# A state-space scan in 64 states: three of four time blocks summed in PSUM instead of two, and one PSUM bank for the other products in the loop

## The reference

```python
xz = rmsnorm(x, rms_w) @ in_proj            # xi | z, 512 channels each
xi = silu(causal_conv4(xi))                 # depthwise, 4 taps
dt, Bm, Cm = split(xi @ x_proj)             # 16 | 16 | 16
delta = softplus(dt @ dt_w + dt_b)
h[t] = exp(delta[t] * A) * h[t-1] + (delta[t] * xi[t]) * Bm[t]    # per channel, per state s = 0..15
y[t] = sum over s of h[t, s] * Cm[t, s]
y = (y + xi * D) * silu(z)
x = x + y @ out_proj                        # then attention and FFN
```

## Time and profile before

| | us |
|---|---|
| three runs | 591.8, 594.72, 595.92 |
| median | 594.72 |
| the profiled execution | 597.62 |
| its span, first to last instruction | 595.8 |
| mean granted TensorE clock of it | 0.899 |

### The profile page before, as it was taken

The page is one execution under the profiler, slowest core; times in us unless marked ns, Lnnn a source line. Parts: engine busy times, 40 slices in busy tenths (PEclk is TensorE's granted clock), DMA queues, the critical chain, the costliest instruction groups (busy, mean ns, idle before and its releaser), DMA issues. The chain is left out here.

```text
span 595.8 us, 7810 instructions
## 1 busy us (share of the span) xinstructions
PE 489.1 (82%) x2733; PEld 346.1 (58%) x2733; DVE 488.7 (82%) x576; ACT 354.8 (60%) x618; POOL 352.9 (59%) x212
## 2 busy tenths in 40 slices
PE   5877898779778999896689998956977777999882
PEld 5522765455566667554566765646866466787631
DVE  4858999997999899989988898899999899732413
ACT  4566667668765767886667678876466476400300
POOL 5007979756885698777938987776577645000000
PEclk9997999976889999779999996899998888796985
DMA  8221101111101011010110111012012910073004
GB/s 289 93 71 56 53 36 36 38 37 35 36 35 36 34 39 39 35 36 36 37 36 35 36 38 37 35 36 71 31 40 86 402 54 1 1 286 129 1 0 147
DMA packets 17919, 38.87 MB, mean 65 GB/s; under 512 B 1666, under 2 KB 10498, under 8 KB 17875
## 3 DMA queue, kind: packets, MB, share of 16 engines
q1 hardware_dynamic: 17874, 38.32, 18.4%
HBM read 36.08 MB, written 2.23 MB: 64 GB/s over the span
## 5 line engine op out<-in xcount | busy, mean ns | idle before, releaser
L1259 POOL TENSOR_TENSOR scanmem<-par,scanmem 128x1024 f32<-128x1024 f32 x128 | 299.3, 2363 | 111.9 <-PE hT L759 64.2
L1130 ACT ACTIVATE dA<-par,Aneg 128x512 f32<-128x512 f32 x256 | 172.5, 690 | 70.7 <-DVE scanmem L1583 69.7
L759 PE MATMUL hT<-con,scanmem 128*128 128x128 f32 x1024 | 160.5, 295 | 57.1 <-DVE yTd L1599 34.7
L759 PEld LDWEIGHTS hT<-con,scanmem 128*128 128x128 f32 x1024 | 123.3, 150 | 116.5 <-DVE yTd L1599 47.4
L1583 DVE TENSOR_TENSOR_SCAN scanmem<-dA,carry,scanmem 128x512 f32<-128x512 f32 x128 | 156.9, 1268 | 2.5 <-ACT dA L1130 2.4
L1583 DVE TENSOR_TENSOR_SCAN scanmem<-dA,scanmem 128x512 f32<-128x512 f32 x128 | 149.3, 1209 | 3.4 <-ACT dA L1130 3.0
L1140 ACT ACTIVATE hc<-hT,CTs 128x512 f32<-128x512 f32 x128 | 87.3, 682 | 77.0 <-PE hT L759 76.3
L1599 DVE SCALAR_TENSOR_TENSOR yTd<-hT,CTs,yTd 128x512 f32<-128x512 f32 x120 | 87.9, 732 | 9.8 <-PE hT L759 9.6
L543 PE MATMUL yacc<-con,hc 128*128 128x128 f32 x512 | 79.1, 298 | 5.8 <-ACT hc L1140 5.8
L487 PE MATMUL pp<-xnT,wi 128*128 128x512 f32 x128 | 66.8, 655 | 7.7 <-ACT xnT L927 4.0
L543 PEld LDWEIGHTS yacc<-con,hc 128*128 128x128 f32 x512 | 65.2, 154 | 9.9 <-ACT hc L1140 6.5
(11 more groups left out here) (169 smaller groups left out, 467.7 us busy)
## 6 DMA issues: line engine op xcount, KB each, us to landing
scanmem<-brow SPq DMA_DIRECT2D x32, 512.0 KB, 3.6
par<-in SPq DMA_DIRECT2D x1, 4096.0 KB, 16.7
scanmem<-in SPq DMA_DIRECT2D x1, 4096.0 KB, 14.5
xt<-in SPq DMA_DIRECT2D x4, 512.0 KB, 6.7
wi<-in SPq DMA_DIRECT2D x2, 1024.0 KB, 7.8
out<-par SPq DMA_DIRECT2D x4, 512.0 KB, 3.9
aw<-in SPq DMA_DIRECT2D x5, 256.0 KB, 6.5
xr<-in SPq DMA_DIRECT2D x1, 1024.0 KB, 9.5
```

Of the source, the lines that this page charges most:

```text
L759: last = nc.tensor.transpose(hT[:, i % 2, m * P:(m + 1) * P], hb[:, n % RING, m, i * P:(i + 1) * P], ident)
L1130: A(dA[:, m % 2, :], delta(c)[:, m, :], ACT.Exp, scale=Aneg[:, m * NS + s:m * NS + s + 1]).then_inc(da_ready, 1)
L1259: nc.gpsimd.tensor_tensor(hb[:, n % RING, ms, :], dx(c)[:, ms, :], Bb[:, row:row + 1, :].to_broadcast([P, 2, T]), ALU.mult).then_inc(bx_re ...
```

## The change

Blocks 0, 1 and 2 are now scaled by ScalarE (three mul_steps a state) and summed by TensorE in three yacc banks (BY_ACT = 3); block 3 alone is summed by VectorE, behind scan 3. mul_step reads hT[i % 2], and the third scaled tile lies in yTd. The Y job of block 1 is gone; the gate products of state 0 are three. The third yacc bank is taken from pp: pp is one bank, and in the loop each job waits for the read of the job before it (held_before). Ahead of the loop the jobs alternate with yacc[2], behind it with dA[1]. The tables move the jobs to other slots.

```diff
-PROLOGUE = {3: [("T", 0), ("T", 1)], 4: [("I", 0)], 5: [("I", 1)], 6: [("I", 2)], 7: [("I", 3)], 8: [("V", 0)],
-            10: [("V", 2)], 12: [("V", 3)], 14: [("X", 0)], 18: [("XT", 0), ("D", 0)], 20: [("D", 1), ("D", 2)], 21: [("D", 3)],
-            22: [("Z", 0)], 23: [("Z", 1)], 24: [("Z", 2)], 25: [("Z", 3)]}
-EPILOGUE = {1: [("Y", 1), ("Y", 3)], 11: [("O", 0)], 16: [("O", 1)], 28: [("R", 0)], 30: [("R", 1)]}
+PROLOGUE = {4: [("T", 0)], 5: [("T", 1)], 6: [("I", 0)], 7: [("I", 1)], 8: [("I", 2)], 9: [("I", 3)], 11: [("V", 0)],
+            13: [("V", 2)], 15: [("V", 3)], 17: [("X", 0)], 18: [("XT", 0)], 19: [("D", 0)], 20: [("D", 1)], 21: [("D", 2)],
+            22: [("D", 3)], 25: [("Z", 0)], 26: [("Z", 1)], 27: [("Z", 2)], 28: [("Z", 3)]}
+EPILOGUE = {1: [("Y", 3)], 2: [("O", 0)], 23: [("O", 1)], 29: [("R", 0)], 31: [("R", 1)]}
...
+def held_before(q):
+
+    if q < LOOP_FIRST or q > TAIL_FIRST + 1:
+        return [ORDER[q - 2]] if q >= 2 else []
+    if q == LOOP_FIRST:
+        return [ORDER[q - 2], ORDER[q - 1]]
+    return [ORDER[q - 1]] if q <= TAIL_FIRST else []
...
-        yacc = ctx.enter_context(nc.psum_tensor("yacc", [P, 2, DI], F32))
-        pp = ctx.enter_context(nc.psum_tensor("pp", [P, 2, 512], F32))
+        yacc = ctx.enter_context(nc.psum_tensor("yacc", [P, BY_ACT, DI], F32))
+        pp = ctx.enter_context(nc.psum_tensor("pp", [P, 512], F32))
...
             def run(job):
-                q = INDEX[job]
-                if q >= 2:
-
-                    pe.wait_ge(job_free[q % 2], q // 2)
+                for earlier in held_before(INDEX[job]):
+                    wait_read(pe, earlier)
...
-                        reduce(n - 1, 0)
-                        reduce(n - 1, 2)
+                        for i in range(BY_ACT):
+                            reduce(n - 1, i)
...
-                A(hc[:, e % 2, :], hT[:, 0, :], ACT.Copy, scale=CTs[:, c % 2, i, s:s + 1]).then_inc(mul_done, 1)
+                A(scaled_tile(i), hT[:, i % 2, :], ACT.Copy, scale=CTs[:, c % 2, i, s:s + 1]).then_inc(mul_done, 1)
...
                     if n:
                         mul_step(n - 1, 0)
+                        mul_step(n - 1, 1)
...
                     scan_step(n, 1)
-                    if n:
-                        mac_step(n - 1, 1)
                     for job in to_read(2 * n):
                         read(job)
                     scan_step(n, 2)
                     scan_step(n, 3)
                     if n:
-                        mac_step(n - 1, 3)
+                        mac_step(n - 1)
```

More of the change, by code:

```diff
@@ L64 @@
 DX_AT = [13, 14]
-POOL_TANH_AT = 11
-POOL_FINISH_AT = 7
+POOL_TANH_AT = 13
+POOL_FINISH_AT = 8
 def product_convs(n):
@@ L106, in all_slots @@
             for m in range(CT):
-                beside[m // 2] += [("Z", 0, m)]
-            beside[4] += [("TP", 0, 0)]
-            beside[6] += [("U", 0, 0)]
+                beside[m] += [("Z", 0, m)]
+            beside[10] += [("TP", 0, 0)]
+            beside[12] += [("U", 0, 0)]
         else:
@@ L342, in bank, with scaled_tile @@
         def bank(job):
-            return pp[:, INDEX[job] % 2, :]
+            q = INDEX[job]
+            if q < LOOP_FIRST:
+                return (pp[:, :], yacc[:, BY_ACT - 1, :])[q % 2]
+            if q >= TAIL_FIRST:
+                return (pp[:, :], dA[:, 1, :])[(q - TAIL_FIRST) % 2]
+            return pp[:, :]
+        def scaled_tile(i):
+            return hc[:, i, :] if i < 2 else yTd[:, 0, 0, :]
         def freed(job):
@@ L558, in job_O @@
                 if j:
-                    for i in (1, 3):
-                        wait_read(pe, ("Y", e, i))
-                pe.wait_ge(gated, 2 * (e + 1))
+                    wait_read(pe, ("Y", e, 3))
+                pe.wait_ge(gated, BY_ACT * (e + 1))
                 if e == 0 and j == 0:
@@ L753, in transposes @@
                     pe.wait_ge(scan_done, CT * (n + 1))
-                e = 2 * n + i // 2
-                if e >= 1:
-                    pe.wait_ge(mac_done if i % 2 else mul_done, e)
+                    if n:
+                        pe.wait_ge(mul_done, BY_ACT * n)
+                elif i == 1:
+                    if n:
+                        pe.wait_ge(mac_done, n)
+                else:
+                    pe.wait_ge(mul_done, BY_ACT * n + i - 1)
                 for m in range(CT):
@@ L830, in general_batch @@
                     for k in range(KD):
-                        last = mm(pp[:, 0, i * NH:(i + 1) * NH], x1T[:, k, i * P:(i + 1) * P], u[:, k, b * NH:(b + 1) * NH], start=k == 0, stop=k == KD - 1)
+                        last = mm(pp[:, i * NH:(i + 1) * NH], x1T[:, k, i * P:(i + 1) * P], u[:, k, b * NH:(b + 1) * NH], start=k == 0, stop=k == KD - 1)
                 did(last)
                 step(pe, b, "g")
-                did(rows_by_heads(b, pp[:, 0, :], a_sb))
+                did(rows_by_heads(b, pp[:, :], a_sb))
                 step(pe, b, "m")
-                did(weight_by_heads(pp[:, 0, :], 1, g_sb))
+                did(weight_by_heads(pp[:, :], 1, g_sb))
                 step(pe, b, "r")
-                did(weight_by_heads(pp[:, 0, :], 2, qD))
+                did(weight_by_heads(pp[:, :], 2, qD))
                 for j in range(2):
@@ L841, in general_batch @@
                     for k in range(KD):
-                        last = mm(pp[0:NH, 0, :], r_sb[:, k, 0, 0:NH], x1T[:, k, j * 512:(j + 1) * 512], start=k == 0, stop=k == KD - 1)
+                        last = mm(pp[0:NH, :], r_sb[:, k, 0, 0:NH], x1T[:, k, j * 512:(j + 1) * 512], start=k == 0, stop=k == KD - 1)
                     did(last)
@@ L848, in general_batch @@
                             t0 = (2 * j + i) * P
-                            last = mm(pp[:, 0, i * DM:(i + 1) * DM], x1T[:, k, t0:t0 + P], aw[:, 3, k, :], start=k == 0, stop=k == KD - 1)
+                            last = mm(pp[:, i * DM:(i + 1) * DM], x1T[:, k, t0:t0 + P], aw[:, 3, k, :], start=k == 0, stop=k == KD - 1)
                     did(last)
@@ L867, in general_batch @@
                     for k in range(KD):
-                        last = nc.tensor.transpose(pp[:, 0, k * P:(k + 1) * P], go[:, k * P:(k + 1) * P], ident)
+                        last = nc.tensor.transpose(pp[:, k * P:(k + 1) * P], go[:, k * P:(k + 1) * P], ident)
                     did(last)
@@ L898, in general_batch @@
                     for k in range(KD):
-                        last = nc.tensor.transpose(pp[:, 1, k * P:(k + 1) * P], gf3[:, k, :], ident)
+                        last = nc.tensor.transpose(dA[:, 1, k * P:(k + 1) * P], gf3[:, k, :], ident)
                     did(last)
@@ L1168, in _ @@
             n = NCH * NS
-            mul_step(n - 1, 0)
-            mul_step(n - 1, 2)
+            for i in range(BY_ACT):
+                mul_step(n - 1, i)
             for job in BESIDE[-1] + TAIL:
@@ L1631, in general_batch @@
                 step(dve, b, "m_out")
-                did(ev_M(None, pp[:, 0, :]))
+                did(ev_M(None, pp[:, :]))
                 with dve.Fori(0, GB) as t:
```

93 lines of the change are left out of this document (45 added, 48 removed).

## The result

The changed kernel takes 686.11 us (median of four runs, 683.95 to 688.61), against 593.26 us (589.07 to 595.92) for the kernel before on the same chip: a ratio of 1.157, with a 95% interval of 1.149 to 1.166. Forecast was 653 us, with a range of 622 to 683. The direction was right, and the loss is over half larger than forecast: 93 us instead of 58. The profiled execution took 684.48 us with a span of 682.6.

A forecast was written before the change was run, and what follows sets the result against it. VectorE was taken as the bound, with TensorE full in some stages. One-bank chains add 49.6 us and the clock 9 to the profiled 597.6, giving 656, or 653 as median; range 622 to 683.

The forecast's parts named there:

- The gain of 42 us that had to be left standing: VectorE loses one 0.65 us sum a state; over 64 states 42 us saved if nothing else moved.
- My rival's figure of 577 for a TensorE bound: Rival: gain stands, 577 us if TensorE's work becomes the bound without holes, 556 if VectorE stays it; chance 0.08 together.
- The chain through the odd slots: Transposes, copies, read, exponentials, copy 2, sum 2, next odd product: product time + 3.77 + read + 0.49 us; V 8.88.
- The rival of a full V stage at 6.6 us a state: Only D and Z reads hold TensorE; the V stage runs full at 6.6 us a state: 633 us, chance 0.17.
- The read of the bank: In the loop a product waits until the one before is read: 2.77 us for D, 1.45 for Z, 1.28 more for firsts.
- the clock: Part of each chunk runs at 1.2 instead of 2.4 GHz: 3 us per chunk in chunks 0 to 2, +9.
- The sum of chunk 2: Chunk 2's slot-by-slot chains at full clock: 135.9 us against 115.3 before, +20.6.
- R1 to Y3: Step of chunk 2's chain, from the R1 product to the Y3 product: one state, 5.5 us.
- Chunk 0: No O and R, but Z in its first four slots and TP and U: 135 us against 122.6, +12.
- Chunk 3 and the tail: Chunk 3: 8 us gained, O0 costs 4 more, adjacent slots 3, so -1; behind the loop one Y product less, -1.
- the signs that I had named: Profile after: V 8.9 us apart, sum 2 waiting about 2, D 5 to 7 apart, scans waiting over 15, chunk 2 136 to 139.
- the holes pull the clock down: Rival for the D and Z part: holes lower TensorE's clock there, 675 to 683 us, chance 0.14.

The follow-up runs named there:

- the tables alone: Kernel before with only the job tables and GpSimd places of the changed kernel, still two pp banks: 612.84 us, ratio 1.027.
- The idle products: Eight unused 128-column identity products ahead of the waits of D1, D3, Z1 and Z3 in chunks 0 to 2, added to the control of after: 669.62 us, ratio 1.125.
- the control of after: Changed kernel with block 2's sum added onto block 0's bank, leaving one PSUM bank unused; bank rule and tables kept: 682.22 us, ratio 1.147.
- the sums alone: Kernel before with three copies and three sums a state, two pp banks, its own tables, block 2 summed into block 0's bank: 589.52 us, ratio 0.989.

## Why the prediction was right in kind and short in size

**The gain of 42 us that had to be left standing** was right as VectorE's work (plain states 5.12 to 5.4) and wrong as a gain. With both banks and the tables of before it brought 1%. My rival's figure of 577 for a TensorE bound was nearer than 556, and still 12 us too good.

**The chain through the odd slots** held to 0.3 us: V products 8.84 us apart against 8.88 forecast, I3 to V0 6.45 against 6.57, X to XT 6.23 against 6.00. Sum 2 waited 1.43 us for the third copy, where I had written about 2. The rival of a full V stage at 6.6 us a state falls. One word of mine was too strong: I called this section "the bank", and the tables alone already give 8.26 us a state with two banks.

**The read of the bank** in D and Z held as well (to 0.4 us) where TensorE's clock was high. The D group in the timeline:

```profile
431.97 0.69 DVE L1415 SCALAR_TENSOR_TENSOR par<-pp,par 128x512 f32<-128x512 f32 x1 [3.20 <-ACT par L1028]
...
432.71 2.07 PE L555 MATMUL pp<-dbc,wdt 17*128 17x512 f32 x2 [4.81 <-DVE par L1415]
...
434.71 1.97 PE L779 MATMUL hT<-con,scanmem 128*128 128x128 f32 x8
...
435.87 0.69 ACT L1157 ACTIVATE yTd<-hT,CTs 128x512 f32<-128x512 f32 x1 [2.82 <-PE hT L779]
...
439.32 1.12 PE L555 MATMUL pp<-dbc,wdt 17*128 17x512 f32 x2 [0.33 <-DVE par L1415]
440.38 1.09 PE L779 MATMUL hT<-con,scanmem 128*128 128x128 f32 x8
...
445.00 2.07 PE L555 MATMUL pp<-dbc,wdt 17*128 17x512 f32 x2 [3.54 <-DVE par L1415]
```

D0 to D1 took 6.95 us (6.73 forecast), D2 to D3 5.68 (5.45). But D1 to D2 took 6.61 where the chain gave 4.96, and this is **the term that was mis-sized: the clock**, which I had put at 9 us. TensorE had stood still for 4.81 us ahead of D1. The granted clock of 431.9 to 438.5 us was 0.50, that is 1.2 GHz in place of 2.4: the product took 2.07 us in place of 1.12 and the transposes behind it 1.97 in place of 1.09. The copy that needs them started 3.16 us after the product, where I had 1.50. The whole of that 1.66 lies on the chain, because the copy, the read, the exponentials and the next product follow from it. D3 to O1 (6.60 against 4.96) is the same pattern. In Z1 to Z2 (6.16 against 4.50) the product itself is slow, 3.57 us in place of 1.88 behind a hole of 3.63, and the transposes behind it are not. I had spread an unchanged share of low clock evenly, 3 us a chunk. In place of that three long holes cost 1.65 us each in chunk 2, at the operations right behind them, 5 us in all. The same count gives 6.4 in chunk 1 (O0 is slow there too) and 11.8 in chunk 0, so about 23 us in place of 9, an estimate from the durations. The 14 us between them are half of the 28 that were missed. The idle products took 8.8 us out of chunks 0 to 2 of the control of after, with D1 still low in chunks 0 and 2; for the D and Z part alone the durations give 15 in three chunks, and the runs show 8 to 9 of it.

A row of the trace before could have told. The D product of the earlier trace rows is itself one of 2.07 us, and I took 0.86 for it. The granted clock of before was 0.50 from 362.8 to 376.0 us, and TensorE had no hole over 0.9 us there; the stretch begins with this row:

```profile
362.81 2.07 PE L535 MATMUL pp<-dbc,wdt 17*128 17x512 f32 x2 [0.20 <-DVE par L1397]
```

**The sum of chunk 2** was 135.9 at full clock and 138.9 with my allowance, and 143.6 was measured. (Z0 to Z1 adds up to 6.27 from its terms, not 6.22, which changes nothing. The +13 a chunk of my upper end does not follow from "half of the chain": TensorE's half of 53 us, at half speed, would be +26.) The difference of 7.7 us to the first is 5.0 for the three places at the lower clock, 1.55 for R1 to Y3, and 1.1 for many small ones of either sign. R1 to Y3 I had set at one plain state, 5.5 us, and it took 7.05: the product of Y3 needs VectorE's sum of block 3 (start 349.62), which stands behind scans 2 and 3, and these behind exponentials that stand behind the read of R1. No row that I had used showed this chain.

**Chunk 0** missed most, 149.4 us against 138. Its first T job starts 25.9 us after its first scan, not 20.4. Its first three Z products stand behind holes of 2.2 to 3.1 us and take 3.4 to 3.6 us in place of 1.88, 5.0 us more in all, and VectorE's counts for the ranks of batch 1 (L1536) stand among their reads. Two of them, and the fourth at full clock:

```profile
56.13 3.64 PE L507 MATMUL pp<-xnT,wi 128*128 128x512 f32 x4 [2.76 <-DVE par L1410]
...
62.88 3.57 PE L507 MATMUL pp<-xnT,wi 128*128 128x512 f32 x4 [2.20 <-DVE par L1410]
...
71.26 1.88 PE L507 MATMUL pp<-xnT,wi 128*128 128x512 f32 x4
```

T0 to T1 (4.84 against 3.19) adds 1.7, and the operations behind D1, D3 and Z1 add 5.1, less the 3 I had allowed; I3 to V2, with TP and U, adds 1.1.

**Chunk 3 and the tail** I had put at 112 and 76 us, and they take 115.7 and 78.6. In chunk 3 the sums alone gave 6.2 us of my 8, the tables alone gave 3.0, where I had put a loss, and the one bank, with Y3, O0 and O1 a slot later, then cost 6.9, where I had 4 for O0. These single differences are rough: chunk 3 also differed by 3.4 us between two kernels that are the same in it.

Chunk by chunk, the misses are 11, 6, 5, 4 and 3 us and make up 28 of the 28.5 us between 656 and the 684.5 of the profiled execution. Of the signs that I had named, the scans' wait for exponentials came out at 13.5 us and not over 15, sum 2 waited 1.43 us and not 2, and chunk 2 was 143.6 us long and not 136 to 139. The others held. My own rival that "the holes pull the clock down" had 675 to 683 at a chance of 0.14; it was the nearest, though its upper end is still 3 us below 686, and it should have had more weight. The read of 4.05 us with its table load was in my own chain, and the hole that it leaves TensorE could have been worked out from it. What TensorE does behind such a hole I priced from an average over chunks, and from no row. The rest of the miss is not of one kind: 3 us in R1 to Y3, twice 1.55, 6 in chunk 3 and the tail, and some 5 in small differences.

**The two rules.** That independent products should rotate through banks (the Trainium skill, Perfetto Trace Analysis, section Optimizing Tensor Performance) is borne out here: one bank in place of two cost 59 us, 48 of them where nothing else had changed. The drain that is added to a table load (the Trainium skill, ScalarE: Activation LUTs, section What ACT_TABLE_LOAD costs) did not show. The load starts where the exponential before it ends, and the next operation starts 1.30 us after the load does:

```profile
52.68 0.69 ACT L1148 ACTIVATE dA<-par,Aneg 128x512 f32<-128x512 f32 x1 [0.42 <-DVE scanmem L1601]
...
53.39 1.28 ACT L1015 ACT_TABLE_LOAD   x1
54.69 0.60 ACT L1015 ACTIVATE par<-pp 128x512 f32<-128x512 f32 x1
```
